# A projection on float16 halves, and a layer's first epilogue moved into the tiles that follow

## The reference

```python
h = max(layernorm(x), 0);  x = x + attention_layer(h, adj, ...)            # "layer 0"
h = max(layernorm(x), 0);  x = x + relu(norm(adj) @ h @ W1 + b)            # layer 1
h = max(layernorm(x), 0);  x = x + relu(adj @ ((h > 0) @ sign(W2).T))      # layer 2
h = max(layernorm(x), 0)
s = h @ W3;                x = x + (1 - t) * s + t * (adj @ s)             # layer 3, "the fourth"
```

## Time and profile before

| | us |
|---|---|
| three runs | 1011.74 to 1013.94, median 1013.07 |
| the profiled execution, its own time | 1012.57 |
| its span in the trace | 1010.6 |
| TensorE busy | 970.5 |
| VectorE busy | 761.2 |
| ScalarE busy | 456.1 |

### The profile page before, as it was taken

The page is one execution under the profiler, slowest core; times in us unless marked ns, Lnnn a source line. Parts: engine busy times, 40 slices in busy tenths (PEclk is TensorE's granted clock), DMA queues, the critical chain, the costliest instruction groups (busy, mean ns, idle before and its releaser), DMA issues.

```text
span 1010.6 us, 20926 instructions
## 1 busy us (share of the span) xinstructions
PE 970.5 (96%) x7625; PEld 713.9 (71%) x7625; DVE 761.2 (75%) x1143; ACT 456.1 (45%) x822; POOL 76.5 (8%) x156
## 2 busy tenths in 40 slices
PE   8879999999999999999997799999999999999996
PEld 8457788888888888888884355555568864555553
DVE  6688899999999999999997665555657765555553
ACT  6576677777667777776768221222210001111111
POOL 4100000000000000000030000000003320000000
PEclk9999999999999999999998799999999999999998
DMA  4802244344324434344022145545554445656662
GB/s 170 116 6 52 19 66 65 28 64 62 60 24 65 64 26 64 57 61 53 0 72 103 34 152 186 201 170 195 175 203 137 165 165 185 208 200 201 211 223 61
DMA packets 36412, 110.38 MB, mean 109 GB/s; under 512 B 4220, under 2 KB 24213, under 8 KB 36245
## 3 DMA queue, kind: packets, MB, share of 16 engines
q1 hardware_dynamic: 27653, 97.94, 28.2%
q0 software_dynamic: 7488, 11.08, 13.8%
q10 hardware_dynamic: 1232, 0.85, 0.3%
HBM read 128.58 MB, written 14.50 MB: 142 GB/s over the span
## 4 chain that ended last, share of the span: by engine, by line
PE 77%; DVE 11%; issue 6%; ACT 3%; DMA 1%; POOL 0%; DVEq 0%; ACTq 0%; POOLq 0%
PE f_ya L1277 35%; PE f_ya L1206 17%; PE f_yb L1206 16%; PE f_yb L1196 5%; DVE f_wm L1476 3%; DVE f_gb L1477 2%; DVE f_s_mat L1482 2%; ACT f_gb L960 1%; PE f_ya L1157 1%; PE f_yb L1190 1%; PE f_yb L1157 1%; DMA f_ident<-ident_dram 1%; ACT f_s_mat L970 1%; PE f_ya L1267 1%; DVE f_s_mat L1487 0%
## 5 line engine op out<-in xcount | busy, mean ns | idle before, releaser
L1206 PE MATMUL f_ya<-f_x_mat,f_s_mat 128*128 128x257 f16 x2028 | 350.8, 272 | 3.6 <-DVE f_x_mat L1457 1.9
L1277 PE MATMUL f_ya<-f_x_mat,f_a 128*128 128x512 f16 x1352 | 323.2, 385 | 9.6 <-DVE f_x_mat L1545 9.6
L1206 PE MATMUL f_yb<-f_x_mat,f_s_mat 128*128 128x257 f16 x2028 | 332.4, 273 | 0.0
L1277 PEld LDWEIGHTS f_ya<-f_x_mat,f_a 128*128 128x128 fp8e4 x1352 | 132.2, 99 | 149.7 <-DVE f_x_mat L1545 15.7
L1206 PEld LDWEIGHTS f_yb<-f_x_mat,f_s_mat 128*128 128x128 f16 x2028 | 195.4, 96 | 27.0
L1206 PEld LDWEIGHTS f_ya<-f_x_mat,f_s_mat 128*128 128x128 f16 x2028 | 149.9, 97 | 21.2 <-issue 4.5
L960 ACT ACTIVATE f_gb<-f_e_tile,f_expc 128x256 f32<-128x256 f32 x338 | 139.7, 493 | 0.0
L970 ACT ACTIVATE f_s_mat<-f_wm 128x1792 f16<-128x1792 f32 (+1 forms) x52 | 82.7, 1590 | 116.0 <-DVE f_wm L1476 97.6
L1209 PE MATMUL f_ya<-f_ones,f_a 128*128 128x1 f16 x676 | 113.0, 167 | 0.0
L1476 DVE TENSOR_TENSOR f_wm<-f_gb,f_a 128x1792 f32<-128x1792 f32 (+1 forms) x52 | 98.1, 1887 | 16.2 <-ACT f_gb L960 14.4
L1622 DVE SCALAR_TENSOR_TENSOR f_gb<-f_gb 128x1664 f32<-128x1664 f32 x52 | 98.0, 1887 | 10.4 <-DVE f_s_mat L1672 10.4
(11 more groups left out here) (148 smaller groups left out, 752.6 us busy)
## 6 DMA issues: line engine op xcount, KB each, us to landing
f_gb<-adj_dram SPq DMA_DIRECT2D x52, 832.0 KB, 5.3
f_a<-f_a_dram SPq DMA_DIRECT2D x39, 832.0 KB, 4.4
f_a<-adj_t_dram POOLq DMA_DIRECT2D x26, 224.0 KB, 4.8
f_a_dram<-f_a SPq DMA_DIRECT2D x26, 224.0 KB, 3.1
f_a<-adj_t_dram POOLq DMA_DIRECT2D x26, 192.0 KB, 5.0
f_a_dram<-f_a SPq DMA_DIRECT2D x26, 192.0 KB, 2.9
out_dram<-f_s_mat SPq DMA_DIRECT2D x25, 128.0 KB, 4.6
f_xs<-x_dram SPq DMA_DIRECT2D x3, 768.0 KB, 9.5
```

The source lines that it names most:

```text
L1206: return pe.matmul(bank[:, 0:F + 1], s_mat[:, j, side, i], x_mat[:, j, x_side, 0:F + 1], start=start, stop=stop)
L1277: return pe.matmul(bank_a[p][:, 0:W], a8_pair[:, r, at:at + P], x_layer[layer][:, j, 0:W], start=(j == 0), stop=(j == TILES - 1))
```

## The change

Seven edits:

- The projection of layer 3 runs on float16: z (scaled by `Z3`) and W3 (scaled by `WT`) are each split into a high half and a low half, and six 128 x 256 float16 matmuls (two 128-row parts, times high x high, high x low, low x high) take the place of the two float32 ones.
- The high half of z is made by ScalarE's copy of the turn; the low half by a new VectorE operation, `low3`, behind `update`. The projection waits for both.
- The halves of W3 are made once: the high one on ScalarE ahead of layer 1, the low one on VectorE at the head of layer 1.
- Two flags more (on the size of W3 and of t) are made at the head of layer 1: eight small VectorE operations.
- `EPILOGUE_AT[3]` is (13, 20) for (13, 19).
- The epilogue of tile 0 is no longer ahead of tile 2: `LATE_AT` puts it at blocks 12 and 20 of tile 2, the turn of tile 1 at block 25 of tile 2, its projection at block 3 of tile 3, and tile 2's at blocks 13 and 20 of tile 3. Tiles 2 to 5 are written out ahead of TensorE's loop.
- Two checks that ran inside the first pair of layer 3 now run ahead of it, so four checks stand before the first `product`.

```diff
-        EPILOGUE_AT = {1: (9, 15), 3: (13, 19)}
+        EPILOGUE_AT = {1: (9, 15), 3: (13, 20)}
+        LATE_AT = ({12: (0, 0), 20: (0, 1), 25: (1, 0)}, {3: (1, 1), 13: (2, 0), 20: (2, 1)})
...
+                a.wait_ge(late_w, 64)
+                a.activation(w3_16[:, 0], w_sb[3], ACT.Copy, scale=WT).then_inc(w3_done, 1)
...
+                        if layer == 3:
+                            a.activation(zt16[:, 0], ep[:, 0:F], ACT.Copy, scale=Z3).then_inc(zt_hi, 1)
...
+                        pe.wait_ge(zt_done[3], t + 1)
+                        for c in range(FB):
+                            for half, w_half in ((0, 0), (0, 1), (1, 0)):
+                                mm = pe.matmul(op[:, 0:F], zt16[:, half, c * P:(c + 1) * P], w3_16[:, w_half, c, :],
+                                               start=(c + half + w_half == 0), stop=(c == FB - 1 and half == 1))
...
-                    if layer != 2:
+                    if layer == 1:
                         layer_epilogue(layer, 0, 0, 0)
                         layer_epilogue(layer, 0, 0, 1, True)
-                    with pe.Fori(0, PAIRS // 2) as k:
+                    apart_pairs = 2 if layer == 3 else 0
+                    for i in range(apart_pairs):
+                        for p in range(2):
+                            tile(1 + i, p, r0 ^ 1 ^ i, 16 + 16 * i, LATE_AT[p] if i == 0 else None)
+                    with pe.Fori(apart_pairs // 2, PAIRS // 2) as k:
...
-                            v.tensor_tensor(xo[:, p, :], o, xt, ALU.add).then_inc(upd[3], 1)
+                            v.scalar_tensor_tensor(xo[:, p, :], o, 1.0 / (WT * Z3), xt, ALU.mult, ALU.add).then_inc(upd[3], 1)
...
+                    def low3(t):
+
+                        v.wait_ge(zt_hi, t + 1)
+                        v.scalar_tensor_tensor(zt16[:, 1], ep[:, 0:F], Z3, zt16[:, 0], ALU.mult, ALU.subtract)\
+                         .then_inc(zt_done[3], 1)
...
                             if layer == 3:
                                 product(t, p)
+                                if first and p == 0:
+                                    low3(0)
                             if not (first and p == 0):
 
                                 update(t - 1, 1 - p, k if p else k - 1, first)
+                            if layer == 3 and not (first and p == 0):
+                                low3(t)
...
-                            if layer == 3 and not (last and p == 1):
+                            if layer == 3 and not first and not (last and p == 1):
                                 check(CHECKS1 + 2 + t, 1 - p)
...
                         check(CHECKS1, 1)
                         check(CHECKS1 + 1, 0)
+                        check(CHECKS1 + 2, 1)
+                        check(CHECKS1 + 3, 0)
                         pair(0, True)
```

More of the change, by code:

```diff
@@ L554, in fast_program @@
         bad = sb("bad", [P, CHECKS])
-        flags = sb("flags", [P, 6])
+        flags = sb("flags", [P, 8])
         den = sb("den", [P, 4])
@@ L647, in fast_program @@
         flw = sem("flw")
+        w3_done = sem("w3_done")
+        zt_hi = sem("zt_hi")
         ex_done = sem("ex_done")
@@ L1084, in turned_copy @@
                         a.wait_ge(zt_psum[layer], t + 1)
-                        a.activation(yt_sb[:, 0:F], ep[:, 0:F], ACT.Copy).then_inc(zt_done[layer], 1)
+                        if layer == 3:
+                            a.activation(zt16[:, 0], ep[:, 0:F], ACT.Copy, scale=Z3).then_inc(zt_hi, 1)
+                        else:
+                            a.activation(yt_sb[:, 0:F], ep[:, 0:F], ACT.Copy).then_inc(zt_done[layer], 1)
                     def pair(k, first):
@@ L1254, in layer_epilogue @@
                             pe.wait_ge(read_o[layer], t)
-                        project(t, op, w_sb[layer], FB, zt_done[layer], p_done[layer])
+                        if layer == 1:
+                            project(t, op, w_sb[layer], FB, zt_done[layer], p_done[layer])
+                            return
+                        if first:
+                            pe.wait_ge(w3_done, 2)
+                        pe.wait_ge(zt_done[3], t + 1)
[3 more added lines that the diff above has]
+                                               start=(c + half + w_half == 0), stop=(c == FB - 1 and half == 1))
+                        mm.then_inc(p_done[3], 1)
                 def sign_turn(t, p):
@@ L1278, in block, with tile @@
                                          start=(j == 0), stop=(j == TILES - 1))
-                    def tile(q, p, r, n):
+                    def tile(q, p, r, n, late=None):
                         t = 2 * q + p
@@ L1290, in tile @@
                                 sign_multiply(t - 2)
-                            if layer != 2 and j in EPILOGUE_AT[layer]:
+                            if late is not None:
+                                if j in late:
+                                    of, part = late[j]
+                                    layer_epilogue(3, of, of % 2, part, (of, part) == (0, 1))
+                            elif layer != 2 and j in EPILOGUE_AT[layer]:
                                 layer_epilogue(layer, t - 1, 1 - p, EPILOGUE_AT[layer].index(j))
@@ L1332, in _ @@
                 pe.wait_ge(flagd, 1)
-                pe.matmul(bank_c[:, 0:1], ones[:], flags[:, 5:6], start=True, stop=True).then_inc(flagd, 1)
+                pe.matmul(bank_c[:, 0:1], ones[:], flags[:, 7:8], start=True, stop=True).then_inc(flagd, 1)
                 layer_epilogue(3, TILES - 1, 1, 1)
@@ L1694, in pair @@
                                 v.tensor_reduce(flags[:, 0:1], bad[:], AX.X, ALU.add).then_inc(flc, 1)
-                                v.wait_ge(flc, 6)
-                                v.tensor_reduce(flags[:, 5:6], flags[:, 0:5], AX.X, ALU.add).then_inc(flagd, 1)
+                                v.wait_ge(flc, 8)
+                                v.tensor_reduce(flags[:, 7:8], flags[:, 0:7], AX.X, ALU.add).then_inc(flagd, 1)
                             if layer == 2:
@@ L1727, in _ @@
                         v.tensor_reduce(flags[:, 4:5], w0_far[:], AX.X, ALU.add).then_inc(flc, 1)
+                        flag_step(v.tensor_reduce(w0_top[:, 0, 0:FB], w_sb[3], AX.X, ALU.max))
+                        flag_step(v.tensor_reduce(w0_top[:, 1, 0:FB], w_sb[3], AX.X, ALU.min))
+                        flag_step(v.scalar_tensor_tensor(w0_top[:, 0, 0:FB], w0_top[:, 1, 0:FB], -1.0, w0_top[:, 0, 0:FB],
+                                                         ALU.mult, ALU.max))
+                        flag_step(v.tensor_scalar(w0_far[:, 0:FB], w0_top[:, 0, 0:FB], WT_MAX, None, ALU.is_gt))
+                        flag_step(v.scalar_tensor_tensor(w0_far[:, 0:FB], w0_top[:, 0, 0:FB], WT_MIN, w0_far[:, 0:FB],
+                                                         ALU.is_lt, ALU.add))
+                        v.tensor_reduce(flags[:, 5:6], w0_far[:, 0:FB], AX.X, ALU.add).then_inc(flc, 1)
+                        flag_step(v.tensor_tensor(w0_top[:, 0, 0:1], t_col[:], t_col[:], ALU.mult))
+                        v.tensor_scalar(flags[:, 6:7], w0_top[:, 0, 0:1], T_MAX ** 2, None, ALU.is_gt).then_inc(flc, 1)
+                        v.wait_ge(w3_done, 1)
+                        v.scalar_tensor_tensor(w3_16[:, 1], w_sb[3], WT, w3_16[:, 0], ALU.mult, ALU.subtract).then_inc(w3_done, 1)
                         with v.Fori(1, PAIRS) as k:
```

5 lines of the change are left out of this document (4 added, 1 removed).

## The result

The changed kernel takes 1015.28 us in the median of 15 runs, 1013.34 for the kernel before beside them; the ratio is 1.0022, interval 1.0014 to 1.0029. Timed again with the experiments it came to 1015.08 and 1.0019 (1.0010 to 1.0027). So it is slower by about 2 us, where I had forecast 4.85. The fifteen times of each kernel lie in two groups: before, five at 1011.5 to 1012.2 and ten at 1013.1 to 1013.9; after, seven at 1013.6 to 1014.5 and eight at 1015.3 to 1016.4. Between like groups the distance is 2.7 to 2.8 us, so the 2 us depend in part on how many executions fell into each; what puts one into a group was not traced. The profiled execution took 1015.86 us, its span 1014.2.

What follows compares the result with a forecast made beforehand. TensorE, busy 970.5 of 1010.6 us, was taken as the bound in layers 1 and 3. The terms +3.3 + 1.7 + 4.2 - 4.6 + 0.25 = +4.85 us on 1012.57 gave 1017.4 us; 8-in-10 range 1015.0 to 1020.6.

Steps and rivals of the forecast that it cites:

- term 3: Head of layer 1: nine added VectorE operations fully paid, +3.3 us, plus a clock fall after TensorE's idling, +1.7 us.
- Term 1, the loop: Layer 3, tiles 4 to 25: six float16 matmuls save 0.21 us per tile, -4.6 us in all.
- The new wait of the projection: Layer 3's loop: `low3` is in time by 0.06 us, so no cost; bound 0.1 us per tile, 2.2 us.
- That rival: Layer 3's loop: `low3` is late in every tile, the sum plus 2.2 us, 1020.1 us; chance 0.1.
- Term 3, the nine operations: Head of layer 1: nine VectorE operations delay TensorE by all their length, +3.3 us, bounds 2.9 and 3.7.
- Term 3, the clock: Head of layer 1: about 3.9 us of TensorE idleness brings half clock, +1.7 us, bounds 0 and 3.1.
- Term 4, the entry: Entry to layer 3: checks awaiting transfers hold product 0; TensorE idles 6.84 us, then half clock and a stall: +4.2 us.
- Term 5, the tail: End of layer 3: nothing hides the last `low3`; less the matmul saving, about +0.25 us, bounds 0.1 and 0.6.
- The rival of covered checks: Entry to layer 3: early transfers let product 0 start as before; -2.85 us, 1010.2 without a layer 1 fall; chance 0.04.
- no clock is lost and the transfer lands early: Layer 1 head has no clock fall and layer 3's entry costs 2.0: +0.8 us, 1013.9 us; chance 0.09.

Runs made afterwards that it cites:

- e7: Kernel before, plus W3's high half and the nine VectorE operations at the head of layer 1, results unused: 1014.83 us, ratio 1.0020.
- e2: The change with the nine operations moved from the head of layer 1 to layer 3, behind its second check: 1013.20 us, ratio 1.0000 to before.
- e10: The change with the nine operations at the head of layer 1 done twice: 1020.96 us, ratio 1.0079 to before.
- e6: The change with layer 3's projection at block 19 instead of 20: 1015.96 us, ratio 1.0023 to before.
- e12: The kernel before, unchanged, profiled once more: span 1012.0 us, against 1010.6 in its first profile.
- e1: The change with the two moved checks put back into layer 3's first pair: 1010.77 us, ratio 0.9973 to before.
- e4: The change with tile 0's epilogue again ahead of tile 2 and only two checks ahead of product 0: 1012.75 us, ratio 0.9992 to before.
- e11: The change itself, unaltered, profiled and timed once more: 1015.08 us, ratio 1.0019 to before.
- e5: The change with 26 unused float32 matmuls keeping TensorE busy at the entry to layer 3: 1013.76 us, ratio 1.0010 to before.
- e8: Kernel before with four checks ahead of layer 3's product 0 and none in its first pair: 1019.52 us, ratio 1.0061.
- e3: The change with the checks back in layer 3's first pair and the nine operations ahead of its product 0: 1007.43 us, ratio 0.9942 to before.

## Why the prediction missed

**The direction was right, and most of the mechanisms; the sum was too high** by a factor above two: +4.85 forecast, +1.9 (medians) to +2.2 (ratio) measured. **The step that failed is term 3, the head of layer 1**: 5.0 us forecast (3.3 for the nine operations, all of it paid, and 1.7 for a fall of the clock), 2.0 to 2.1 by the times of e7 and e2. That is 2.9 to 3.0 too much, as much as the whole miss (2.7 to 2.9), and the clock charge is the larger part of it. The errors in the other terms, up to 0.8 us each and of both signs, about cancel, which is luck.

- *Term 1, the loop*: forecast -4.6, the marks give -4.33 (142.92 against 147.25), within 0.02 us the same in each trace with the float16 projection but e10's (142.67). The row of layer 0's stream was the right row: a steady tile saves the 0.21 us forecast, and the missing 0.24 is one tile, tile 4, which takes 6.73 (6.48 in e10). The estimate of -6.2 from the sustained spacing in the Trainium skill ("TensorE: Matmul & The Clock Gate", Back-to-back issue gap) was off.
- *The new wait of the projection*: no cost, as said, and with more room than 0.06 us: `low3` takes 0.42, and e6 takes away one block (0.216) without a wait. That rival falls.
- *Term 3, the nine operations*: forecast 3.3. The first pair of traces has 2.84, the second 1.9. I had counted a hand-over behind each of the small ones, but some begin before the one ahead has ended. And by time they cost 2.0 (e7) and 2.1 (e2). **I took TensorE's own readiness at the turn of the signs from one execution**, as if it never moved. It moves with how long the half clock at the head of layer 1 lasts (e12), and where it lasts long, 0.9 us of the nine is covered. So "all of their length is paid" does not hold in every execution.
- *Term 3, the clock*: forecast +1.7, 0 in every trace taken, and little by the times: with the 1.9 to 2.84 that the nine cost by themselves, 2.0 to 2.1 leave no room for 1.7 in most executions. The charge came from one pair of rows: 3.93 us of idleness, and a fall. The wait turned out 3.41 us in two traces (3.40 in e1) and 0.9 to 2.0 us in five (e4 to e7, e11), and no fall followed. With 5.12 us (e10) it did. Length alone doesn't decide: the fall came 2.1 us after the stop in e6 and 4.7 us after it in e10, so two waits of 3.41 without one may be chance. I had charged the fall in full, and allowed for none only in a rival that also needed an early transfer (0.09).
- *Term 4, the entry*: forecast +4.2, measured +3.98 and, in the second pair of profiles, +3.4 (22.81 against 19.40). Product 0 behind the second transfer, 6.67 us of idleness (6.84 said), the half clock, and a stall at block 3 that is 0.3 and not 0.4. e1, e5 and e8 show its shares: without the checks the entry is 2.2 us shorter than before instead of 4.0 longer.
- *Term 5, the tail*: forecast +0.25. It is +0.2 where the last projection meets full clock (e1 and e5, 4.48 and 4.49 against 4.31) and +1.05 where it meets half (both profiles of the change). I had no clock charge in this term.

With what the experiments give the sum is 2.1 + 3.4 to 4.0 - 4.3 + 0.2 to 1.05 = +1.4 to +2.8, which holds the measured 2.2 (1.4 to 2.9). The low end takes the tail at full clock, which neither profile of the change has. The second pair of traces by itself has +1.9 + 3.4 - 4.3 + 1.1 = +2.1.

The rival of covered checks needed transfers of under 2 us; they took 4.3 and 6.3. e1 lets product 0 start as before in another way, and is 2.7 us faster than before, where the rival had -2.85. That agreement is luck in part: by e1's trace the terms are +2.8 - 2.2 - 4.3 + 0.2 = -3.5. The rival "no clock is lost and the transfer lands early" was half right, about the clock of term 3; the transfer landed as late as said.

The change holds two gains (the projection, 4.3 us, and the epilogue in the tiles, about 2) and two costs that are not needed for them. e3 keeps both gains: 6 us faster than before.

## What to carry to other kernels

When work is moved "out of the way" ahead of a layer, look at what released its inputs: here two checks of 2 us each brought the wait for their transfers with them onto the one operation that the bound engine waits for. One-time set-up goes where its engine waits anyway (VectorE ahead of product 0, 3.65 us), not into a chain the bound engine already waits on. A charge that falls due in some executions and not in others, such as a fall of the clock in a wait, needs a chance of its own in the sum, and a wait near the bound engine should be read in more than one profiled execution.

## What was not expected of the hardware

- Two executions of the change differ by 2.5 us in what TensorE waits for at the second turn of the signs (3.41 and 0.9), though that turn comes 18.3 us after the restart in both. The half clock at the layer's head lasts until 573 to 574 in the first profile of before and until 579 in the second. Where TensorE is behind at half clock, extra work on VectorE is partly free.
- A wait of 3.41 us of TensorE left the granted clock at full (the change, e1), while waits of 3.66 (e8, head of layer 1), 3.93 (before) and 5.12 us (e10) were followed by half. But the fall itself came as early as 2.1 us after the stop (e6) and as late as 4.7 (e10), behind full work at full clock both times, so these runs give no length that is safe.
- Filling such a wait with matmuls that nothing uses kept the clock up in both places tried, and the blocks behind ran in 2.6 us instead of 4.8 (e5).
- Tile 4 of layer 3 takes 6.72 to 6.74 us in all traces with the float16 projection but e10's (6.48), where later tiles take 6.49; with the float32 projection it doesn't stand out (6.69). In the change VectorE's second product operation started 0.54 us late there (no releaser but itself), and TensorE's turn was held by 0.2 us. What causes it stays open.
